# Second-layer gelus carried into the next block's session in an attention and feed-forward kernel on one core

## The reference

```
x = layernorm(x + attention(x))     # 16 heads of 8, rms-normed and rotated q and k, softmax, projection
h = silu(x @ w1 * s1) * (x @ w2 * s2)        # 128 -> 512
h = gelu(h @ h1 * t1)                        # 512 -> 512, "first hidden layer"
h = gelu(h @ h2 * t2)                        # 512 -> 512, "second hidden layer"
x = layernorm(x + h @ w3 * s3)               # 512 -> 128
```

## Time and profile before

| | |
|---|---|
| median of 3 runs | 366.97 us (365.79 to 366.97) |
| the profiled execution: its own time | 367.24 us |
| its span, first to last instruction | 365.1 us |
| PE busy | 336.8 us, 92% |
| ACT busy | 308.4 us, 84% |
| DVE busy | 215.1 us, 59% |
| POOL busy | 30.4 us, 8% |
| mean granted clock of TensorE | 0.989 of full |

### The profile page before, as it was taken

One profiled execution on the slowest core, in us unless ns is written; L12 is line 12 of the kernel. 1 busy time (PEld: TensorE's weight loads), 2 busy tenths in 40 slices (PEclk: granted clock), 3 DMA queues, 4 the chain that ended last, 5 costly groups with the idle time before them and its releaser, 6 DMA issues.

```text
span 365.1 us, 6179 instructions
## 1 busy us (share of the span) xinstructions
PE 336.8 (92%) x2107; PEld 137.2 (38%) x2107; DVE 215.1 (59%) x449; ACT 308.4 (84%) x364; POOL 30.4 (8%) x48
## 2 busy tenths in 40 slices
PE   8999999997999989999999899998999898899980
PEld 3432223222322444443222445332323542267760
DVE  3998978775357634464466453554477262078853
ACT  3899999899999889789999897989998987965440
POOL 5032212002100000002100000012000000010011
PEclk9999999999999999999999999999999999999995
DMA  7939744326221300303030300204031100000002
GB/s 225 303 120 321 214 163 172 135 84 251 83 71 37 102 0 2 102 2 105 27 102 0 102 0 13 90 0 134 0 104 53 49 2 0 3 0 0 2 1 63
DMA packets 14844, 29.52 MB, mean 81 GB/s; under 512 B 2704, under 2 KB 7200, under 8 KB 14816
## 3 DMA queue, kind: packets, MB, share of 16 engines
q1 hardware_dynamic: 11104, 17.02, 15.7%
q0 software_dynamic: 3280, 11.82, 9.0%
q10 hardware_dynamic: 432, 0.33, 0.3%
HBM read 17.65 MB, written 9.44 MB: 74 GB/s over the span
## 4 chain that ended last, share of the span: by engine, by line
PE 67%; ACT 15%; DVE 9%; issue 5%; DMA 1%; POOL 1%; ACTq 0%; POOLq 0%; DVEq 0%
PE ps L583 24%; PE ps L630 14%; ACT probs L1022 13%; PE ps L569 11%; PE ps L779 4%; PE ps L620 4%; PE ps L533 2%; DVE ffn L1284 2%; DMA mean<-in_means 1%; PE ps L684 1%; PE ps L847 1%; PE ps L738 1%; PE ps L600 1%; PE ps L545 1%; DVE ffn L1281 1%
## 5 line engine op out<-in xcount | busy, mean ns | idle before, releaser
L1022 ACT ACTIVATE probs<-ps 128x1024 f32<-128x1024 f32 x256 | 242.2, 1039 | 20.6 <-PE ps L569 20.1
L583 PE MATMUL ps<-probs,va 128*9 128x512 f32 x896 | 113.0, 594 | 6.1 <-ACT probs L1022 4.5
L569 PE MATMUL ps<-qa,ka 32*128 32x512 f32 x512 | 75.9, 494 | 5.4 <-ACT probs L1022 5.0
L569 PEld LDWEIGHTS ps<-qa,ka 32*128 32x128 f32 x512 | 31.0, 181 | 101.8 <-ACT probs L1022 61.0
L1284 DVE TENSOR_SCALAR ffn<-ps,col 128x512 f32<-128x512 f32 x34 | 25.5, 750 | 51.6 <-PE ps L630 47.6
L630 PE MATMUL ps<-g_hi,w_hi 128*128 128x512 f32 x96 | 40.4, 421 | 1.2 <-DVE ffn L1284 0.8
L630 PE MATMUL ps<-g_lo,w_hi 128*128 128x512 f32 x96 | 37.7, 393 | 0.0
L583 PEld LDWEIGHTS ps<-probs,va 128*9 128x9 f32 x896 | 15.6, 89 | 50.8 <-issue 26.4
L630 PEld LDWEIGHTS ps<-g_hi,w_hi 128*128 128x128 f32 x96 | 18.0, 187 | 13.0 <-issue 4.3
L1259 DVE TENSOR_TENSOR g_lo<-ffn,g_hi 128x512 fp32r<-128x512 f32 x32 | 22.1, 692 | 1.1
L630 PEld LDWEIGHTS ps<-g_lo,w_hi 128*128 128x128 f32 x96 | 18.1, 188 | 3.1
(11 more groups left out here) (171 smaller groups left out, 354.2 us busy)
## 6 DMA issues: line engine op xcount, KB each, us to landing
ka<-k_scr SPq DMA_DIRECT2D x56, 128.0 KB, 2.8
k_scr<-parts POOLq DMA_DIRECT2D x8, 512.0 KB, 4.0
q_scr<-parts POOLq DMA_DIRECT2D x8, 512.0 KB, 4.5
qa<-q_scr SPq DMA_DIRECT2D x56, 64.0 KB, 2.2
va<-v_all SPq DMA_DIRECT2D x14, 144.0 KB, 2.1
ffn<-in_h POOLq DMA_DIRECT2D x1, 1024.0 KB, 9.8
h_raw<-in_h POOLq DMA_DIRECT2D x1, 1024.0 KB, 7.6
xT<-in_x_t SPq DMA_DIRECT2D x3, 256.0 KB, 6.3
```

Of the source, the lines that this page charges most:

```text
L569: mm = pe.matmul(s_tile(u)[:, i, :], ka[rows, slot, kt * P:(kt + 1) * P], qa[rows, slot, :], start=True, stop=not shifted)
L583: mm = pe.matmul(ps[32 * h:32 * h + VW, O_BANK, :], v, probs[:, step % 4, h, :], start=(kt == 0), stop=(kt == KT - 1))
L1022: nc.scalar.activation(probs[:, step % 4, 2 * pair:2 * pair + 2, :], s_tile(u), ACT.Exp).then_inc(exp_done, 1)
```

## The change

- The second layer's gelus of block b are no longer done in chunk b+1 but in chunk b+2, at the head of the session behind step 20; the session behind step 26 is gone. Each of chunks 1, 2 and 3 has one session. In chunks 2 and 3 it is two gelus of 1024 columns (of block c-2) and four of 512 (of block c-1).
- The second layer's pieces 0, 1 and 2 stand in slots 44, 48 and 52; piece 3 is carried to slot 1 of the next chunk (behind the last values of the chunk before). Of block 2, pieces 0 and 1 stand in chunk 3 and the rest at the end, as before.
- Splits of the second layer (slots 45, 46, 49, 50), the w3 product (56) and the turn, norm and store (59) are those of block c-2. So chunk 1 has none of them, and chunk 3 now has them for block 1.
- Tiles of their own for what is carried (in space that is free by then: `pre_2`, `second_o`, `rest_hi`, `rest_lo`, a second x1).
- Steps 25 and 29 no longer hold their values, and the seven unread matmuls are gone.
- The three chunks are written out on PE, ACT and DVE, with constant counts. `from_tiles` waits for each input tile in every piece.
- At the end `rest_sum` moves behind the first three of the w3 products of block 3 (input tile 1, high part), and on DVE `rest_norm` moves behind the two half splits of the last tile, `rest_shift` behind the two scalings of y (L1611).
- On POOL the order of inverse roots follows, with the same instructions.

```diff
@@ constants
-HELD_LAST = (2, 14, 18, 19, 20, 22)
-WARM_STEPS = {28: 7}
-HIDDEN_SLOTS = ((33, 36, 40, 42), (44, 48, 51, 52))
-GELU_STEPS = (20, 26)
-HELD_STEPS = (2, 14, 18, 19, 20, 22, 25, 29)
-SPLIT_SLOTS = ((42, 42, 42, 43), (52, 52, 54, 55))
+HIDDEN_SLOTS = (33, 36, 40, 42)
+SECOND_SLOTS = (44, 48, 52)
+CARRIED_SLOT = 1
+SESSION_STEP = 20
+PAIRED = ((0, 1), (2, 3))
+HELD_STEPS = (2, 14, 18, 19, 20, 22)
+SPLIT_SLOTS = (42, 42, 42, 43)
+SECOND_SPLIT_SLOTS = (45, 46, 49, 50)
...
+def second_pieces(c):
+    return HM - 1 if c < NCH - 1 else REST_FROM
@@ POOL
             def finish(c):
-                rsqrt(2 * c)
                 rsqrt(2 * c + 1)
+                rsqrt(2 * c + 2)
                 pool.wait_ge(y_ready, c + 1)
...
+            rsqrt(0)
             with pool.Fori(0, NCH - 2) as c:
                 finish(c)
-            rsqrt(2 * (NCH - 2))
@@ PE
-            def ffn_at(base, c, slot, passes, last):
+            def ffn_at(base, c, slot, passes):
+                b = c - 1
+                if slot == CARRIED_SLOT and b:
+                    hidden(base, b - 1, 1, HM - 1, passes)
...
+                if slot in SECOND_SLOTS[:second_pieces(c)]:
+                    hidden(base, b, 1, SECOND_SLOTS.index(slot), passes)
+                if slot == DOWN_SLOT and b:
+                    down(base, b - 1, passes)
+                if slot == Y_SLOT and b:
+                    y_transpose(base, b - 1)
...
                     logits(c, step, 0, shifted)
-                    if passes and step in WARM_STEPS and not last:
-                        pe.wait_ge(mix_free, base + use[0])
-                        keep_warm(WARM_STEPS[step])
                     logits(c, step, 1, shifted)
...
                         if layer == 1 and m == 1:
                             rest_projection(passes)
-                        if layer == 1 and m == 2:
-                            rest_sum()
...
+                        if (k, part) == (1, 0):
+                            rest_sum()
                         if (k, part) in ((1, 1), (2, 0)):
...
-                with pe.Fori(1, NCH - 1) as c:
+                for c in range(1, NCH):
                     chunk(c, passes, shifted)
-                chunk(NCH - 1, passes, shifted, last=True)
@@ ACT
+            def second_gelu(c):
+                act.wait_ge(second_pre, HM * (c + 1))
+                for tiles in PAIRED:
+                    cols = slice(tiles[0] * CH, (tiles[-1] + 1) * CH)
+                    nc.scalar.activation(second_o[:, cols], pre_2[:, cols], ACT.Gelu).then_inc(second_act, 1)
...
-                    if step in GELU_STEPS[:sessions]:
-                        gelu(c - 1, GELU_STEPS.index(step))
+                    if step == SESSION_STEP:
+                        if c >= 2:
+                            second_gelu(c - 2)
+                        for m in range(HM):
+                            gelu(c - 1, m)
@@ DVE
+                if slot == CARRIED_SLOT and b:
+                    second_pre_activation(base, b - 1, HM - 1)
...
+                if slot in SECOND_SLOTS[:second_pieces(c)]:
+                    second_pre_activation(base, b, SECOND_SLOTS.index(slot))
+                if slot in SECOND_SPLIT_SLOTS and b:
+                    second_gelu_split(cb, b - 1, SECOND_SPLIT_SLOTS.index(slot))
+                if slot == DOWN_SLOT and b:
+                    scale_y(base, b - 1)
+                if slot == Y_SLOT and b:
+                    finish(base, cb, b - 1)
...
                     if layer == 1 and m == 2:
                         rest_scale()
-                        rest_norm()
                     last_split_tile(layer + 1, m)
...
-            rest_shift()
             hi, lo = last_tile(2, HM - 1)
...
+            rest_norm()
             for hf in range(2):
                 dve.wait_ge(last_ready, R_DOWN + hf + 1)
                 nc.vector.tensor_scalar(half_of(yT, hf), ...).then_inc(last_given, 1)
+            rest_shift()
```

More of the change, by code:

```diff
@@ L115, with mix_uses @@
 TILE_OF = tiles_in_turn(TILE_SWAPS)
-def gelu_count(layer, i):
-    return HM + sum(len(GELU_TILES[n]) for n in range(layer)) + i + 1
+def second_pieces(c):
+    return HM - 1 if c < NCH - 1 else REST_FROM
+def mix_uses(c):
+    return 2 + 2 * HM + HM + second_pieces(c) + (3 if c >= 2 else 0)
 def wait(eng, sem, count):
@@ L644, in y_transpose @@
                 mm.then_inc(mix_ready, 1)
-            def ffn_at(base, c, slot, passes, last):
+            def ffn_at(base, c, slot, passes):
+                b = c - 1
+                if slot == CARRIED_SLOT and b:
+                    hidden(base, b - 1, 1, HM - 1, passes)
                 if slot == PROJ_SLOT:
-                    project(base, c)
+                    project(base, b)
                 if slot == X_SLOT:
-                    x_transpose(base, c)
+                    x_transpose(base, b)
                 if slot in UP_SLOTS:
[L653 to L660, removed]
+                    up(base, b, UP_SLOTS.index(slot), passes)
+                if slot in HIDDEN_SLOTS:
+                    hidden(base, b, 0, HIDDEN_SLOTS.index(slot), passes)
+                if slot in SECOND_SLOTS[:second_pieces(c)]:
[4 more added lines that the diff above has]
+                    y_transpose(base, b - 1)
             def first_task(n):
@@ L825, in turned @@
                         keep_warm(after[hf], 2)
[L827 removed]
+                pe.wait_ge(mix_free, use[0])
                 rest_piece(2, (0, 1), passes)
@@ L1047, in _, with chunk @@
             act.preload_act_table_set("exp_and_others")
-            def chunk(c, sessions):
+            def chunk(c):
                 for step in range(STEPS):
@@ L1299, in gate, with gelu_split @@
                 split_tile(cb, m).then_inc(g_ready, 1)
-            def gelu_split(cb, c, layer, m):
-                i = next(i for i, tiles in enumerate(GELU_TILES[layer]) if m in tiles)
-                dve.wait_ge(act_done, ACTS * c + gelu_count(layer, i))
+            def gelu_split(cb, c, m):
+                dve.wait_ge(act_done, ACTS * c + HM + m + 1)
                 split_tile(cb, m).then_inc(g_ready, 1)
@@ L1331, in ffn_at @@
                     if slot == GATE_SLOTS[m]:
-                        gate(cb, c, m)
-                for layer in range(2):
-                    if slot in HIDDEN_SLOTS[layer] and not (last and layer == 1 and HIDDEN_SLOTS[1].index(slot) >= REST_FROM):
-                        m = HIDDEN_SLOTS[layer].index(slot)
-                        pre_activation(base, m, (C_H1, C_H2)[layer], any(m == tiles[-1] for tiles in GELU_TILES[layer]))
-                    for m in range(HM):
-                        if slot == SPLIT_SLOTS[layer][m] and not (last and layer == 1):
-                            gelu_split(cb, c, layer, m)
-                if slot == DOWN_SLOT and not last:
-                    scale_y(base, c)
-                if slot == Y_SLOT and not last:
-                    finish(base, cb, c)
+                        gate(cb, b, m)
+                if slot in HIDDEN_SLOTS:
+                    pre_activation(base, HIDDEN_SLOTS.index(slot), C_H1, True)
+                for m in range(HM):
+                    if slot == SPLIT_SLOTS[m]:
+                        gelu_split(cb, b, m)
+                if slot in SECOND_SLOTS[:second_pieces(c)]:
[6 more added lines that the diff above has]
+                    finish(base, cb, b - 1)
             def late_products(n):
@@ L1453, in first_chunk, with chunk @@
                 assert use[0] == MIX_FIRST
-            def chunk(c, base, cb, last=False):
+            def chunk(c, base, cb):
+                begun = use[0]
                 for step in range(STEPS):
                     g, kt = divmod(step, KT)
-                    ffn_at(base, cb, c - 1, 2 * step, last)
+                    ffn_at(base, cb, c, 2 * step)
                     if kt == 0 and g:
@@ L1500, in _ @@
                     row_maxima(n)
-            start = links[0]
-            with dve.Fori(1, NCH - 1) as c:
-                use[0], links[0] = 0, 0
-                chunk(c, MIX_CHUNK * (c - 1) + MIX_FIRST, CHAIN_CHUNK * (c - 1) + start)
-                assert use[0] == MIX_CHUNK and links[0] == CHAIN_CHUNK, links[0]
-            use[0], links[0] = 0, 0
-            c, base, cb = NCH - 1, MIX_CHUNK * (NCH - 2) + MIX_FIRST, CHAIN_CHUNK * (NCH - 2) + start
-            chunk(c, base, cb, last=True)
-            assert use[0] == LAST_MIX
+            cb = 0
+            for c in range(1, NCH):
+                chunk(c, 0, cb)
             def rest_low(m):
                 dve.wait_ge(rest_high, m + 1)
-                nc.vector.tensor_tensor(rest_lo[:, m, :], pre_a[:, m * CH:(m + 1) * CH], rest_hi[:, m, :].bitcast(F32),
+                nc.vector.tensor_tensor(rest_lo[:, m, :], pre_2[:, m * CH:(m + 1) * CH], rest_hi[:, m, :].bitcast(F32),
                                         ALU.subtract).then_inc(rest_split, 1)
```

88 lines of the change are left out of this document (50 added, 38 removed).

## The result

The changed kernel takes 362.33 us (median of four, 362.32 to 362.53) against 366.97: a ratio of 0.9869, 95% interval 0.9826 to 0.9913, so 4.6 us less. A second set of six runs gave 362.66 and 0.9889 (0.9865 to 0.9914). The forecast was 364.2 with a range of 361.0 to 367.2: the direction and the range hold, the gain is 1.7 times the one forecast. The profiled execution took 362.53 us with a span of 360.4, where before it was 367.24 and 365.1.

The account below looks back on a forecast made before the run. In the chunks, ACT's work plus gaps ended by PE's logits was taken to bound the time. Chunks -1.6 and end -1.1 sum to -2.7 us, from a median of 366.97 to 364.2, range 361.0 to 367.2.

Parts of the forecast that it names:

- The ledger of ACT: Account of ACT's time in the chunks: work removed, gaps removed and gaps added, each gap ended by PE's logits.
- slot 1: Carried piece at the start of chunks 2 and 3: ACT waits 1.85 us, 1.95 with a late pair 8.
- slot 52: New piece behind step 26 in chunks 1 and 2: a gap of 1.75 us on ACT.
- w3 in chunk 2: w3 product in slot 56 of chunk 2: next exponential at 316.33 instead of 315.18, a gap of 1.15 us.
- the 0.72 inside it: Session behind step 20: fourth first-layer gelu's wait for its evacuation, forecast to disappear behind the 2.0 us of added gelus.
- POOL's store: Store of block 1, now at the end of chunk 3 ahead of the inverse roots: forecast hidden, by 1.5 us.
- rivals of the gaps: Five new placements each cost their full 2.04 us and DVE's norm delays the end's scaling: 367.0 us; chance 0.25.
- of the overlap: PE regains its lead or pieces fall into waits; half of the 10 us of gaps does not come: about 360; chance 0.13.
- of no change: A wait counted as hidden takes the place of the loads: within 1 us of 367; chance 0.05.
- The chunks: Chunks 1, 2 and 3 change by -5.4, -1.05 and +4.9 us, in sum -1.6.
- The end: Moving the sum and norm of the rest saves 1.1 us after chunk 3, bounds 0 and -1.8.
- The clock: Rival: clock falls in steps 27 to 31 of chunks 1 and 2 without unread matmuls: 369 to 372 us; chance 0.05.

## Why the prediction was right, and where it was off

**What held.** The ledger of ACT was the right account. The gaps came where they were put: slot 1, 1.85 forecast and 1.78 measured; slot 52, 1.75 forecast, 1.53 and 1.54 measured; w3 in chunk 2, 1.15 and 1.31; w3 in chunk 3, 1.5 and 1.35. The session grew by 1.1 where 1.3 was forecast, and the 0.72 inside it went. The loads cost 1.28 each with no drain (a load at 207.34, the gelu at 208.63); the 2.66 us that the Trainium skill gives for a switch ("ScalarE: Activation LUTs", section "What ACT_TABLE_LOAD costs") are not seen on this kernel. POOL's store stayed hidden. The rivals of the gaps, of the overlap and of no change fall with these rows.

**The chunks, -1.6 forecast and -2.6 measured.** No single term is far off; four small ones lie on the same side. The session grew by 1.1 and not by 1.3, in two chunks (0.4 to 0.5). The gap behind step 26 of chunk 1 was 1.53 and not 1.75 (0.2). The 14 exponentials from pair 50 of chunk 1 took 13.0 without that gap, and not 13.2 (0.2). Up to pair 50 of chunk 1 the loop was worth 0.5 and I took 0.4; with the rounding that is 58.7 for 58.9 (0.2). Up to pair 50 the chunks took 58.7, 61.9 and 61.7 where I had 58.9, 61.95 and 61.95, and from there 14.5, 16.2 and 14.7 where I had 14.95, 16.2 and 14.7.

One constant was misread. I took 0.94 us from one exponential to the next, which is the length of a row divided by its count (3.77 / 4). The row's length holds one whole exponential of 1.03, so the pace without waits is 0.916: (9.27 - 1.03) / 9 in the row of 166.10 before, and (11.11 - 1.03) / 11 in the row of 152.94. It did little harm, because the chunks have many small waits: the 14 exponentials of 305.90 before have a mean of 0.93.

**The end, -1.1 forecast and -2.15 measured.** The two scalings came 1.56 earlier: the sum behind the w3 products takes 1.7 us and not the 1.9 that I added, and the half gelus no longer wait. The other 0.6 of this profile lies behind the issue of the last store, a term that the sum did not have. It differs by up to 1 us between profiles with one and the same end, so a part of it is luck. By the medians the end is worth 2.1, almost twice the forecast, and it is the term that was mis-sized most.

**The clock, right for a reason that was only half seen.** I gave the clock 0.05 and argued from chunk 3, which runs without the matmuls. That was the right comparison for the changed kernel, since neither has a session behind step 26. But I put the matmuls into the ledger of chunks 1 and 2 only as work, and there they were a cover: without them the kernel before is 1.0 to 1.4 us slower. The Trainium skill says in "TensorE: Matmul & The Clock Gate", section "Part 1: The HAM clock gate", that the clock halves when TensorE has been idle. The profiles agree in kind: PE without work for 1.56 and for 3.48 us, then 0.50. They also show that it is not a matter of the wait's length alone: the clock fell behind a wait of 1.88 us and not behind one of 1.86 in the same kernel, and behind one of 1.20 at the start of chunk 1 in one profile and not in two others. The carry removes the wait behind step 26, and with it the need for the cover. It does not rule out every fall: one of the six executions of the second set had a mean granted clock of 0.982 and took 364.20 us.

**How the 4.6 us divide.** Loop and end: 2.7 (363.97 from 366.70). Carry and matmuls: 1.6 (362.33 from 363.97, in two calls; the 0.3 that is missing is what before differed by between the calls). The profiles agree: the chunks fell from 230.3 to 229.2 by the loop and to 227.7 by carry and matmuls, the end by 2.15. The title edit by itself, the carry, gains nothing until the cover is taken away.

## What to carry to other kernels

Before filler matmuls are taken out, look for the wait that they fill, and take the two out together; each alone can be slower. Look at the granted clock of every execution as well: where a fall comes in some executions and not in others, one profile shows only one of the two cases. A function-table session costs its two loads, and if the other engine runs out of work during it, it can cost a stretch at half clock as well (1.4 us here): put sessions where PE has pieces to make up. A piece costs what PE's lead does not cover, so it is cheapest where PE is ahead, and dearest behind a product that waits for the last exponential.

## What the runs showed of the hardware that was not expected

The granted clock fell under the work that followed a wait of 1.56 us in a stretch that was otherwise dense, and doubled the gap behind it (1.38 to 2.94 in chunk 1). Waits of about the same length (1.86 and 1.88 us) were followed by a fall in one place and by none in the other. The 256 KB store at the end landed 2.3 to 2.4 us behind its issue with the new order and 3.9 to 4.6 with the old one, although the stores are issued closer together (1.3 instead of 3.1 us apart); the cause is open, and no time hung on it here.
